# Layer 3's experts in tiles of 256 slots, with weights fetched and split per tile

## What is computed

```python
    def _L3_ffn_ref(x, w1, b1, w2, b2, gate_w, gate_b, expert_biases):
        E = 8
        K = 2
        ...
        scores = xf @ gate_w + gate_b
        gate_probs = jax.nn.sigmoid(scores)
        _, topk_idx = jax.lax.top_k(scores + expert_biases, K)
        ...
        for e in range(E):
            h = jax.nn.relu(xf @ w1[e] + b1[e])
            out = out + combine[:, e:e + 1] * (h @ w2[e] + b2[e])
```

## Time and profile before

| | |
|---|---|
| median of the runs | 2525.2 us |
| the profiled execution | 2520.35 us |
| its span, first to last instruction | 2518.5 us |
| granted TensorE clock, mean of the span | 0.932 of full |
| TensorE busy | 2202.9 us, 87% |
| VectorE / ScalarE / GpSimd busy | 1485.0 / 1054.8 / 675.0 us |
| routing of layer 3 | about 1853.5 to 1918.5 us |
| experts of layer 3 | 1918.5 to 2518.5 us |

### The profile page before, as it was taken

The page is one execution under the profiler, slowest core; times in us unless marked ns, Lnnn a source line. Parts: engine busy times, 40 slices in busy tenths (PEclk is TensorE's granted clock), DMA queues, the critical chain, the costliest instruction groups (busy, mean ns, idle before and its releaser), DMA issues. The chain is left out here.

```text
span 2518.5 us, 45274 instructions
## 1 busy us (share of the span) xinstructions
PE 2202.9 (87%) x13876; PEld 1528.2 (61%) x13877; DVE 1485.0 (59%) x3335; ACT 1054.8 (42%) x2135; POOL 675.0 (27%) x820
## 2 busy tenths in 40 slices
PE   6969688999976999599994679999847999999997
PEld 4858533444455889599992234444624666666765
DVE  2868757888745767366655978888465222222222
ACT  3434344666633443255552336666420222222222
POOL 1424101222200000188870012222001333333332
PEclk8989797999997999799996879999969999999999
DMA  3000042221103000665553422121075222221221
GB/s 118 1 0 0 7 123 64 57 55 49 40 5 102 1 1 1 176 114 115 98 71 100 106 75 54 51 56 40 1 285 150 34 33 33 32 32 32 33 33 26
DMA packets 134683, 151.29 MB, mean 60 GB/s; under 512 B 32777, under 2 KB 118578, under 8 KB 134194
## 3 DMA queue, kind: packets, MB, share of 16 engines
q1 hardware_dynamic: 105394, 110.06, 14.8%
q0 software_dynamic: 29184, 39.87, 10.3%
HBM read 95.47 MB, written 53.87 MB: 59 GB/s over the span
## 5 line engine op out<-in xcount | busy, mean ns | idle before, releaser
L1401 ACT ACTIVATE L_attn_probs<-L_attn_ps_t 128x512 f32<-128x512 f32 x640 | 374.8, 598 | 245.6 <-PE L_attn_ps_t L1325 240.3
L2522 ACT ACTIVATE L_experts_hiddenT<-L_experts_ps_t,L_experts_b 128x128 f32<-128x128 f32 x576 | 156.3, 382 | 485.7 <-PE L_experts_ps_t L2482 485.7
L1308 PE MATMUL L_attn_ps_m<-L_attn_k,L_attn_q 96*128 96x512 bf16 (+3 forms) x1024 | 282.7, 315 | 37.0 <-DMA L_attn_k<-L_k_parts 30.3
L1271 POOL TENSOR_SCALAR_AFFINE_SELECT L_attn_probs<-L_attn_probs 128x512 f32<-128x512 f32 x256 | 153.3, 635 | 469.5 <-ACT L_attn_probs L1401 469.5
L2491 PE MATMUL L_experts_ps_y<-L_moe_w,L_experts_hiddenT 128*128 x1152 | 260.7, 379 | 2.5 <-ACT L_experts_hiddenT L2522 2.5
L2472 PE MATMUL L_experts_ps_h<-L_moe_w,L_experts_tokenT 128*128 x576 | 260.9, 596 | 0.9 <-issue 0.9
L1308 PEld LDWEIGHTS L_attn_ps_m<-L_attn_k,L_attn_q 96*128 96x128 bf16 x1024 | 101.6, 99 | 242.5 <-issue 73.0
L1325 PE MATMUL L_attn_ps_t<-L_attn_q,L_attn_k 98*128 98x512 bf16 (+3 forms) x1024 | 244.4, 300 | 2.8 <-ACT L_attn_probs L1401 2.3
L2491 PEld LDWEIGHTS L_experts_ps_y<-L_moe_w,L_experts_hiddenT 128*128 128x128 f32 x1152 | 213.3, 190 | 29.3 <-issue 3.3
L2541 DVE COPY L_experts_hidden<-L_experts_ps_h 128x1024 f32<-128x1024 f32 x72 | 88.1, 1223 | 241.3 <-PE L_experts_ps_h L2472 241.3
L1441 DVE TENSOR_REDUCE L_attn_top<-L_attn_ps_m 128x1 f32<-128x512 f32 x256 | 175.2, 685 | 63.1 <-PE L_attn_ps_m L1310 61.9
(11 more groups left out here) (428 smaller groups left out, 5003.3 us busy)
## 6 DMA issues: line engine op xcount, KB each, us to landing
L_attn_q<-L_q_parts SPq DMA_DIRECT2D x64, 192.0 KB
L_attn_q<-L_q_parts SPq DMA_DIRECT2D x64, 128.0 KB
L_moe_rows<-L_moe_ln_normed SPq DMA_DIRECT2D x16, 512.0 KB, 3.0
L_moe_w<-L_ffn_w SPq DMA_DIRECT2D x2, 4096.0 KB, 17.9
L_moe_w<-L_ffn_w SPq DMA_DIRECT2D x8, 1024.0 KB, 10.8
L_q_parts<-L_qkv_q_parts SPq DMA_DIRECT2D x32, 192.0 KB, 2.9
L_q_parts<-L_qkv_parts SPq DMA_DIRECT2D x32, 192.0 KB, 3.1
load_ring<-x SPq DMA_DIRECT2D x8, 512.0 KB, 4.1
```

The costliest lines, as they stand in the source:

```text
L1271: return pool.affine_select(out=block, in_=block, compare_op=ALU.is_ge, fill=0.0, base=0, pattern=columns, channel_multiplier=-1)
L1308: pe.matmul(bank[:, at:at + width], q[j][0:96, head, qb * P:(qb + 1) * P], k[j][0:96, 0:width], start=True, stop=False)
L1401: act.activation(probs[j % 2][:, place[unit], :], ps_t[:, n % 2, :], ACT.Exp, scale=scale).then_inc(exped, 1)
L2522: last = act.activation(hiddenT[:, c, :], ps_t[:, c, :], func, bias=b1[:, ds(e, 1), c])
```

## The change

Layer 3's slots lie in 39 tiles of 256, the pairs of each expert padded to a whole tile (9984 slots where there were 9216). `staged_experts` takes the place of `experts`, with the split products of layer 2's form. The first weights are the stationary operand, so the hidden values come out turned and the 8 transposes fall away. There is no room for all weights in two parts, so for each tile SyncE fetches its expert's 2 MB from DRAM into one of two staging buffers, and they are split anew for each tile: ScalarE makes the high part of `w1`, VectorE its low part, GpSimd the high part of `w2` (a copy with conversion), VectorE its low part. The bias loads, the weights of tile 0 and the copy of x into the output are issued during `route` instead. GpSimd's copies of single index columns (L2417, L2428) are gone; the loops are written out instruction by instruction.

```diff
-SLOT_TILES = {2: E * ROOM, 3: 2 * TOK // P + E}
-DUMMY_ROWS = {2: ROOM * P, 3: P}
+FF3 = 1024
+EXPERT_TILES = 39
+ROWS3 = 2 * P
+SLOT_TILES = {2: E * ROOM, 3: EXPERT_TILES * ROWS3 // P}
+DUMMY_ROWS = {2: ROOM * P, 3: 2 * P}
...
-                        did(dve.tensor_scalar(padded_i[:, :], padded_i[:, :], -P, None, ALU.bitwise_and))
+                        did(dve.tensor_scalar(padded_i[:, :], padded_i[:, :], -ROWS3, None, ALU.bitwise_and))
...
+                        did(dve.tensor_scalar(small[:, 1, 0:1], small[:, 1, 0:1], float(ROWS3), None, ALU.max))
...
-def experts(net, layer, rows, total, w1, w2, tables):
...
+class Staged:
+    def __init__(self, net, ctx):
+        self.net = net
+        sb = lambda name, shape, dt=F32: net.sb(f"L3_staged_{name}", shape, dt, ctx)
+        self.w1 = [sb(f"w1_{j}", [P, KC, FF3]) for j in range(2)]
+        self.w2 = [sb(f"w2_{j}", [P, FF3 // P, C]) for j in range(2)]
+        self.b1, self.b2 = sb("b1", [P, E, FF3 // P]), sb("b2", [P, E, C])
+        self.w1_in = net.dram["L3_ffn_w1"].rearrange("e (k p) f -> p e k f", p=P)
+        self.w2_in = net.dram["L3_ffn_w2"].rearrange("e (j p) c -> p e j c", p=P)
+    def early_loads(self, total):
+        net = self.net
+        bias = [(self.b1[:, e, :], net.dram["L3_ffn_b1"][e].rearrange("(j p) -> p j", p=P)) for e in range(E)]
+        bias += [(self.b2[:, e, :], net.dram["L3_ffn_b2"][e].partition_broadcast(P)) for e in range(E)]
+        return ([(self.w1[0][:, :, :], self.w1_in[:, 0]), (self.w2[0][:, :, :], self.w2_in[:, 0])] + bias
+                + [(total[0:TOK, :].rearrange("(u p) c -> p u c", p=P), net.x[:, :, :]),
+                   (total[TOK:TOK + 2 * P, :].rearrange("(u p) c -> p u c", p=P), net.x[:, 0:2, :])])
+def staged_experts(net, rows, total, tables, staged):
...
+    CH = 2
+    W = CH * P
+    NS = EXPERT_TILES
+    RING = 8
+    GIVEN = 4
+    PAIRS = FC // 2
...
+                for i in range(1, NS):
+                    e = expert_of(sp, i)
+                    if i >= 2:
+                        sp.wait_ge(w1_low, KC * (i - 1))
+                    sp.dma_start(staged.w1[i % 2][:, :, :], staged.w1_in[:, ds(e, 1)].rearrange("p a k f -> p (a k) f")
+                                 ).then_inc(w1_in[i % 2], 16)
+                    if i >= 2:
+                        sp.wait_ge(w2_low, KC * (i - 1))
+                    sp.dma_start(staged.w2[i % 2][:, :, :], staged.w2_in[:, ds(e, 1)].rearrange("p a j c -> p (a j) c")
+                                 ).then_inc(w2_in[i % 2], 16)
             @block.gpsimd
             def _(pool):
...
+                def scatter(i):
+                    for s in range(CH):
+                        t = i * CH + s
+                        pool.wait_ge(y_done, t + 1)
+                        if i and s == 0:
+                            for before in (t - 2, t - 1):
+                                pool.wait_ge(added[before % GIVEN], 16 * (before // GIVEN + 1))
+                        pool.indirect_dma_start(out=total, out_offset=bass.IndirectOffsetOnAxis(
+                            ap=tables.give[:, t:t + 1], axis=0), in_=result[t % GIVEN][:, :], in_offset=None,
+                            compute_op=ALU.add).then_inc(added[t % GIVEN], 16)
+                def split_w2(i):
+                    p, half = i % 2, FC // KC
+                    if i:
+                        pool.wait_ge(w2_in[p], 16 * ((i + 1) // 2))
+                    if i >= 2:
+                        pool.wait_ge(y_ready, i - 1)
+                    for k in range(KC):
+                        at = slice(k * half, (k + 1) * half)
+                        pool.tensor_copy(w2[p][0][:, at, :], staged.w2[p][:, at, :]).then_inc(w2_high, 1)
+                for t in range(RING):
+                    gather(t)
+                split_w2(0)
+                for i in range(NS):
+                    if i + 1 < NS:
+                        split_w2(i + 1)
+                    for s in range(CH):
+                        if i * CH + s + RING < NS * CH:
+                            gather(i * CH + s + RING)
+                    scatter(i)
...
+                def product(out, left, right, first, last):
+                    (left_high, left_low), (right_high, right_low) = left, right
+                    pe.matmul(out, left_low, right_high, start=first, stop=False)
+                    pe.matmul(out, left_high, right_high, start=False, stop=False)
+                    return pe.matmul(out, left_high, right_low, start=False, stop=last)
...
+                def up(i):
+                    p = i % 2
+                    pe.wait_ge(x_low, i + 1)
+                    for j in range(FC):
+                        if i and j % 2 == 0:
+                            pe.wait_ge(relu_done, FC * (i - 1) + j + 2)
                         for k in range(KC):
+                            if j == 0:
+                                pe.wait_ge(w1_low, KC * i + k + 1)
+                            last = product(ps_h[:, j, :], cut(w1[p], every, k, slice(j * P, (j + 1) * P)),
+                                           cut(xT[p], every, k, every), k == 0, k == KC - 1)
+                        last.then_inc(h_ready, 1)
+                def down(i):
+                    p = i % 2
+                    if i >= 2:
+                        pe.wait_ge(biased_ready, i - 1)
+                    pe.wait_ge(w2_low, KC * (i + 1))
+                    for t in range(CH):
+                        for j in range(FC):
+                            if t == 0 and j % 2 == 0:
+                                pe.wait_ge(h_low, PAIRS * i + j // 2 + 1)
+                            last = product(ps_y[p][:, t, :], cut(hT[p], every, j, slice(t * P, (t + 1) * P)),
+                                           cut(w2[p], every, j, every), j == 0, j == FC - 1)
                     last.then_inc(y_ready, 1)
+                turn_x(0)
+                turn_x(1)
+                up(0)
+                for i in range(NS):
+                    if i + 1 < NS:
+                        up(i + 1)
+                    if i + 2 < NS:
+                        turn_x(i + 2)
+                    down(i)
             @block.scalar
             def _(act):
+                def split_w1(i):
+                    p = i % 2
+                    if i:
+                        act.wait_ge(w1_in[p], 16 * ((i + 1) // 2))
+                    if i >= 2:
+                        act.wait_ge(h_ready, FC * (i - 1))
+                    for k in range(KC):
+                        act.activation(w1[p][0][:, k, :], staged.w1[p][:, k, :], ACT.Copy).then_inc(w1_high, 1)
+                def split_x(i):
+                    act.wait_ge(x_turned, i + 1)
+                    if i >= 2:
+                        act.wait_ge(h_ready, FC * (i - 1))
+                    act.activation(xT[i % 2][0][:, :, :], ps_x[:, :, :], ACT.Copy).then_inc(x_high, 1)
+                def activate(i):
                     e = expert_of(act, i)
+                    for h in range(PAIRS):
+                        act.wait_ge(h_ready, FC * i + 2 * h + 2)
+                        if i:
+                            act.wait_ge(h_low, PAIRS * (i - 1) + h + 1)
+                        for j in (2 * h, 2 * h + 1):
+                            act.activation(full[:, j, :], ps_h[:, j, :], ACT.Relu, bias=staged.b1[:, ds(e, 1), j]
+                                           ).then_inc(relu_done, 1)
+                        if i >= 2 and h == 0:
+                            act.wait_ge(y_ready, i - 1)
+                        act.wait_ge(relu_done, FC * i + 2 * h + 2)
+                        act.activation(hT[i % 2][0][:, 2 * h:2 * h + 2, :], full[:, 2 * h:2 * h + 2, :], ACT.Copy
+                                       ).then_inc(h_high, 1)
+                split_w1(0)
+                split_x(0)
+                split_x(1)
+                split_w1(1)
+                activate(0)
+                for i in range(NS):
+                    if i + 2 < NS:
+                        split_w1(i + 2)
+                    if i + 1 < NS:
+                        activate(i + 1)
+                    if i + 2 < NS:
+                        split_x(i + 2)
             @block.vector
             def _(dve):
+                def split_w1(i):
+                    p = i % 2
+                    for k in range(KC):
+                        dve.wait_ge(w1_high, KC * i + k + 1)
+                        dve.tensor_tensor(w1[p][1][:, k, :], staged.w1[p][:, k, :], w1[p][0][:, k, :].bitcast(F32),
...
+                def split_h(i):
+                    high, low = hT[i % 2]
+                    for h in range(PAIRS):
+                        at = slice(2 * h, 2 * h + 2)
+                        dve.wait_ge(h_high, PAIRS * i + h + 1)
+                        dve.tensor_tensor(low[:, at, :], full[:, at, :], high[:, at, :].bitcast(F32), ALU.subtract
+                                          ).then_inc(h_low, 1)
...
+                split_w1(0)
```

(15 more changed lines are left out.)

289 lines of the change are left out of this document (85 added, 204 removed).

## The result

The changed kernel takes 2417.57 us in the median of 4 runs (2411.06 to 2419.28), the kernel before, run beside it, 2526.06 us. The ratio is 0.9562, with a 95% interval of 0.9537 to 0.9587: 4.4% faster, and 4.6 us above the forecast of 2413. The profiled execution took 2411.06 us, with a span of 2409.4 us where before had 2518.5.

What follows compares the result with a forecast made beforehand. TensorE bounds layer 3's experts at 11.9 us per 256 slots: +1.8 start, stage 466.1 against 581.4 (-115.3), +1.8 end make -111.7 us; from the median 2525.2, 2413 us. Forecast 2406 to 2422 (66%); 8 in 10: 2403 to 2458.

Steps and rivals of the forecast that it cites:

- the start at half clock: Start of layer 3's expert stage: half clock costs 5.32 us against 3.44 before, given as +2.0 us.
- Rival 3: GpSimd's conversion costs 2.40 us, half of 4.8 us felt on VectorE: about 14 us per tile, +82, 2495 us; chance 5%.
- rival 4: GpSimd's conversion at 2.40 us, all of it blocking VectorE: 15.1 us per tile, +125, 2538 us, slower than before; chance 4%.
- about 0.7 us of it is felt, inside the slack: VectorE per expert tile: GpSimd's copies mostly fall where VectorE waits for ScalarE; the token low has 2.7 us of slack.
- My schedule: Hand-ordered engine queues for one expert tile: GpSimd's high parts from 4.9 to 7.6 us, VectorE waiting for ScalarE between pairs.
- 2 x 1.27 = 2.5 us: Expert tile: each GpSimd copy can hold a VectorE subtraction for about its own length, making VectorE 12.3 us without idle.
- The zero in the sum: Forecast total: the lock between GpSimd's copies and VectorE adds nothing; 0.9 us per tile went into a rival instead.
- The sign that was named for the lock: Profile of the changed kernel: the spread of VectorE's hidden and weight lows, minimum against median, shows the lock.
- the sum would be the rival's: Expert stage: by the skill's rule of VectorE and GpSimd locking each other out, GpSimd's copies work against the change.
- The step that failed: Routing's end to first up: two gathers and splits through ScalarE and VectorE, less the index copies, add 0.8 us.
- Rival 1: VectorE partly bounds the expert stage at 12.3 to 13.3 us per tile, middle 12.8: +35, 2448 us; chance 18%.
- Rival 2: Expert weights land late, over 13 us from issue; at 16 us of landing, 13.4 per tile, +58, 2471 us; chance 6%.

Runs made afterwards that it cites:

- experiment 9: Changed kernel, but at the start SyncE holds w2 of tile 1 and later weights until four gathers land, w1 going at once: 2413.76 us, ratio to before 0.9564.
- experiment 1: Changed kernel, but ScalarE instead of GpSimd makes the high part of the second weights: 2418.07 us, ratio to the kernel before 0.9579.
- experiment 2: Changed kernel, but the down product leaves out hidden high x second weights low, 84 instead of 100 matmuls per tile: 2408.1 us, ratio to before 0.9548.
- experiment 4: Changed kernel plus two spare subtractions of 512 per tile on VectorE: 2450.71 us, ratio to the kernel before 0.9713.
- experiment 3: As experiment 2, but GpSimd fills the second weights' high part with a constant instead of copying it: 2363.56 us, ratio to the kernel before 0.9368.
- Experiment 8: Changed kernel, but SyncE holds all weights of tile 1 and after until four gathers have landed: 2418.95 us, ratio to the kernel before 0.9584.
- experiment 6: As experiment 3, but SyncE issues the load of w1(i+1) ahead of the wait for w2(i): 2341.03 us, ratio to the kernel before 0.9281.

## Why the prediction was right, and where it was off

**The beat.** Forecast 11.84 to 12.1 us for 256 slots, taken 11.9; measured 11.95, with TensorE never idle. Reading it from layer 2's stretch of the same instruction form carried the whole forecast. Products alone start 0.120 us apart, the "about 0.12" that the text allowed. The stage from the first up to the end of the last down product (2397.35 + 0.28) takes 467.6 us against 581.4: -113.8, where the forecast had -115.3. Of the 1.5 us between them, 39 beats at 0.05 us more are +1.9; that leaves 1.6 us for the start at half clock, where 2.0 were given.

**ScalarE, GpSimd, DMA.** ScalarE took 8.0 us per tile (289.92/430 x 11.95), forecast 9.0: its rows overlap a little, two ReLUs in 0.82 to 0.84 us rather than 0.94. The conversion on GpSimd took 2.61 us for a pair, 1.3 each, forecast 1.27 with 2.40 as the other end; which leaves nothing of rivals 3 and 4. That 1.27 was so near is partly luck: a pair whose first has no VectorE subtraction of two SBUF inputs beside it takes 2.03 us (experiment 9, at 1936.03) and one beside VectorE's weight lows 4.00, so 1.3 is a price with some of the lock in it. GpSimd was busy for 9.5 us per tile where the forecast's pieces make 7.8 without the gaps, since scatters and gathers were priced at 1.60 and 1.02 and took 2.3 and 1.5. DMA share 0.74, forecast 0.8.

**VectorE.** It was mis-sized: forecast near 82% busy, measured 95%. Its own work is 9.2 us (experiment 1), forecast 9.8; but the step "about 0.7 us of it is felt, inside the slack" failed: 2.2 us of busy time per tile was the lock (11.4 less 9.2). My schedule put the copies where VectorE waits for ScalarE. In the trace they start behind scatters that had grown from 1.6 to 2.3 us and fall into a pair of hidden lows. The upper end that the prediction drew from layers 0 and 1, 2 x 1.27 = 2.5 us, was the better price. The zero in the sum stayed right by a quarter to half a microsecond of slack per tile, not by the 1.4 that 9.8 + 0.7 would have left, and that is luck: the argument behind it did not hold. Experiments 2 and 4 show the price as soon as the slack is used up. The sign that was named for the lock, minimum against median, would have missed it (676 and 685 ns): about one hidden low in four is held, and held long (37 of 156, at least 2.5 us each), so it stands in the mean. The Trainium skill (SBUF — State Buffer, Who interferes with whom) says that a VectorE instruction with two SBUF inputs and a GpSimd instruction that reads SBUF lock each other out, and that one which only writes does not: experiments 1 and 3 agree with both halves, 691 and 689 ns against 1315. The prediction added that by this rule the sum would be the rival's; the rule held and the sum was not the rival's, since the slack took the lock up.

**The start.** This is the term that was off most. Routing grew by 1.05 us (64.28 to 65.33), forecast +1. From there to the first up the forecast had +0.8 and the trace +4.1. The step that failed counts the gathers and splits but not what SyncE's queue does in the same microseconds: before, only the small bias loads went out there; now the weights of tile 1 and the first ones of tile 2 go out at 1919.0 to 1921.7 and the gathers share the DMA engines with them. Experiment 8 shows it: without them the start is 8.40 us, +0.0. TensorE's order puts both turn_x(0) and turn_x(1), four gathers, ahead of the first up. In the trace tile 0's token low is done at 1928.53 and the first up starts at 1930.03, so this order costs at most 1.5 us there; an order with turn_x(1) behind it was not run.

**The end.** From the last down product to the end of the span it is 11.8 us, 10.5 before: +1.3, forecast +1.8.

**The sum.** +1.05, +4.1, -113.8, +1.3 make -107.3; the layers ahead of the routing ended 1.7 us earlier in this execution, which is no part of the change, and the spans differ by -109.1. The forecast was -111.7. The two misses that count are the start (3.3 us) and the stage (1.5 us), both of one sign; the 1.7 us, which no term of the forecast stands for, hide a part of them in the difference of the spans.

**The rivals.** Rival 1 was real and only a quarter to half a microsecond per tile away: experiment 2 gives VectorE's bound as 11.68, experiment 4 crosses it. Its sum is wrong as it stands: 9.8 us of work, 1 to 2.5 of lock and 0.5 of gaps make 11.3 to 12.8 per tile, not 12.3 to 13.3. The bound of 11.68 (9.2 of work, 2.2 of lock, 0.3 of gaps) lies inside the right sum and outside the one that was written; the 12.8 taken as its middle is the upper end, 1.1 us more than there is. Rival 3's 14 us does not follow from its terms either (9.8 + 2.4 + 0.5 = 12.7); with conversions of 1.3 us nothing hangs on it. Rival 2's loop exists too: ScalarE's wait of 78.4 us in the changed kernel (2.2 us per tile) is its sign, inside ScalarE's own slack, and it was next in line once VectorE was free (10.6 against 10.02). The forecast of that rival laid it to landing times of 13 us and more. Landing was 5.1/6.5/8.0 us (shortest, median, longest), and 5.0/7.5/11.1 in experiment 3, where the loop sets the beat: never 13, and experiment 6 shows the late issue to be the cause. The schedule by hand had given the load 11 us from its issue until ScalarE wants it; in the trace it is 5.8 (issued at 2203.14, ScalarE free at 2208.89).

**Nothing better found.** No variant beats the changed kernel by more than the measurement can tell, since all that compute the whole sit at TensorE's 11.9 us. Experiment 1's split on ScalarE costs no time and leaves up to 2.7 us of room on VectorE in place of 0.5 or less; with experiment 6's queue order it would be what a version with less TensorE work needs. That is an argument; the two together were not run.

## What to carry to other kernels

Take the new beat of the bounding engine from a stretch of the trace that already runs the same instruction form without a gap, and count instructions; that was right to 0.5%. Then price the others against that beat with the worst case of every lock in, because an engine that is 95% busy and costs nothing today is the bound after the next improvement, as VectorE was in experiment 2: adding work to it, or taking work from the bounding engine, shows in one run how far away it is. Look at the mean and the longest of a group, not only at its median, when you look for such a lock. At a seam, list what every queue issues in those microseconds, not only the chain that you follow; and where a load is late, try its place in the queue before its size.

## What the hardware showed that I had not expected

- Scatters (indirect DMAs issued on GpSimd) took 2305 ns and gathers 1500 in this stage, 1601 and 1019 in layer 2. It is not the weights' traffic: 2303 ns for scatters with a third of the bytes moving. It is at least in part VectorE's subtractions with both inputs in SBUF: 1911 ns in the mean when half of the weights' were replaced by a fill, 1.55 to 1.57 us with VectorE idle.
- One hidden low part could be held through both copies of a pair: two of them took 4.35 us where two cost 1.28 to 1.37 alone; the longest single one was 3812 ns. GpSimd is held as well: its pair of conversions took 2.03 us without such a subtraction beside the first of them, 2.61 in the steady stretch and 4.00 beside the weights' lows.
- Gathers of 128 rows beside 3 MB of weights: the first was turned 5.8 us after its issue, 5.7 beside 1 MB, 2.9 without them.
